# Two-layer post-norm transformer: routed experts as 23 blocks of scattered rows in place of all experts for all tokens

## What is computed

```python
x = _layernorm(x + retention(x))                       # 8 heads, decay mask, group norm, gate
x = _layernorm(x + sigmoid(x@Q(w1).T) * (x@Q(w2).T) @ Q(w3).T)   # ternary weights, 704 hidden
x = _layernorm(x + causal_softmax_attention(x))        # 16 heads of 16
# the last one, where the change is:
probs = softmax(x @ W_router.T)                        # 8 experts
rw, sel = top_k(probs, 2)
combine = zeros((T, E)).at[arange(T)[:, None], sel].add(rw)
shared_out = (silu_and_mul(x @ Ws_gate_up, 704) @ Ws_down) * sigmoid(x @ W_sgate.T)
h = silu_and_mul(einsum('th,ehi->eti', x, We_gate_up), 176)
eo = einsum('eti,eih->eth', h, We_down)
sparse_out = einsum('eth,te->th', eo, combine)         # six of eight coefficients are zero
x = _layernorm(x + shared_out + sparse_out)
```

## Time and profile before

| | us |
|---|---|
| median of 3 runs (464.0 to 464.99) | 464.88 |
| the profiled execution | 466.61 |
| its span, first to last instruction | 464.9 |
| TensorE matmuls busy | 394.7 (85%) |
| VectorE busy | 295.4 (64%) |
| ScalarE busy | 204.4 (44%) |
| GpSimd busy | 110.2 (24%) |
| mean granted TensorE clock | 0.911 |

### The profile page before, as it was taken

The page is one execution under the profiler, slowest core; times in us unless marked ns, Lnnn a source line. Parts: engine busy times, 40 slices in busy tenths (PEclk is TensorE's granted clock), DMA queues, the critical chain, the costliest instruction groups (busy, mean ns, idle before and its releaser), DMA issues.

```text
span 464.9 us, 7904 instructions
## 1 busy us (share of the span) xinstructions
PE 394.7 (85%) x3034; PEld 243.1 (52%) x3034; DVE 295.4 (64%) x656; ACT 204.4 (44%) x386; POOL 110.2 (24%) x150
## 2 busy tenths in 40 slices
PE   0958987777789877887997869999899999999996
PEld 0435656534546422233474335656446777777675
DVE  4483357976774993356469975734557968656754
ACT  4576446556126404696762044335563323222421
POOL 2345455445331001565200011012220000000000
PEclk9977889889959865899998579999999999999999
DMA  7940000133000000122000000000000000000001
GB/s 227 368 146 1 1 1 2 45 92 89 3 1 2 0 1 0 57 88 62 1 1 0 1 1 1 2 0 1 1 2 0 1 13 2 11 24 2 1 13 34
DMA packets 6856, 15.14 MB, mean 33 GB/s; under 512 B 738, under 2 KB 4130, under 8 KB 6818
## 3 DMA queue, kind: packets, MB, share of 16 engines
q1 hardware_dynamic: 6820, 14.65, 9.8%
HBM read 13.60 MB, written 1.05 MB: 32 GB/s over the span
## 4 chain that ended last, share of the span: by engine, by line
PE 58%; DVE 22%; ACT 9%; issue 6%; POOL 4%; DMA 1%; POOLq 0%; DVEq 0%
PE psum_a L640 24%; PE psum_b L640 10%; DVE arena_mixers L1290 8%; PE psum_a L776 5%; PE psum_b L848 3%; ACT arena_mixers L1050 2%; PE psum_a L838 2%; PE psum_a L880 1%; DVE arena_ffn L1332 1%; PE psum_b L830 1%; PE psum_a L875 1%; PE psum_a L647 1%; PE psum_b L788 1%; PE psum_b L760 1%; DVE arena_ffn L1329 1%
## 5 line engine op out<-in xcount | busy, mean ns | idle before, releaser
L640 PE MATMUL psum_a<-cut_weights,x_transposed 128*128 128x352 f16 (+3 forms) x774 | 134.9, 327 | 13.3 <-DVE cut_weights L1115 11.9
L640 PEld LDWEIGHTS psum_a<-cut_weights,x_transposed 128*128 128x128 f16 x774 | 75.1, 101 | 62.6 <-DVE cut_weights L1115 12.5
L1406 POOL TENSOR_TENSOR ln_rstd<-ln_var_eps,minus_half 128x1 f32<-128x1 f32 x32 | 19.7, 615 | 196.6 <-DVE ln_var_eps L1106 196.6
L1065 ACT ACTIVATE arena_ffn<-psum_a 128x352 f32<-128x352 f32 x48 | 22.3, 465 | 86.8 <-PE psum_a L640 86.8
L1423 POOL TENSOR_SCALAR_AFFINE_SELECT arena_mixers<-arena_mixers 128x256 f32<-128x256 f32 (+1 forms) x48 | 25.2, 529 | 98.0 <-ACT arena_mixers L1050 97.9
L1290 DVE TENSOR_REDUCE arena_mixers<-psum_a 128x2 f16<-128x768 f32 (+3 forms) x44 | 47.0, 1127 | 2.1 <-PE psum_a L822 2.1
L640 PE MATMUL psum_b<-cut_weights,arena_ffn 128*128 128x256 f16 (+1 forms) x408 | 46.7, 273 | 0.0
L1050 ACT ACTIVATE arena_mixers<-psum_a 128x1024 f32<-128x1024 f32 (+2 forms) x48 | 41.7, 880 | 8.0 <-PE psum_b L640 4.1
L640 PEld LDWEIGHTS psum_b<-cut_weights,arena_ffn 128*128 128x128 f16 (+1 forms) x408 | 39.1, 98 | 6.8 <-issue 1.7
L1329 DVE SCALAR_TENSOR_TENSOR arena_ffn<-arena_ffn,psum_a 128x352 f32<-128x352 f32 x48 | 24.9, 519 | 25.7 <-ACT arena_ffn L1065 14.4
L1332 DVE SCALAR_TENSOR_TENSOR arena_ffn<-arena_ffn,router,psum_a 128x176 f32<-128x176 f32 (+1 forms) x80 | 31.9, 433 | 1.7
(11 more groups left out here) (171 smaller groups left out, 640.4 us busy)
## 6 DMA issues: line engine op xcount, KB each, us to landing
stage<-in_wup SPq DMA_DIRECT2D x8, 512.0 KB, 3.6
stage<-in_wdown SPq DMA_DIRECT2D x4, 512.0 KB, 4.1
arena_ffn<-in_w SPq DMA_DIRECT2D x1, 1408.0 KB, 7.2
stage<-in_xT SPq DMA_DIRECT2D x2, 512.0 KB, 4.2
stage<-in_wqkvg SPq DMA_DIRECT2D x2, 512.0 KB, 5.2
residual<-in_x SPq DMA_DIRECT2D x2, 512.0 KB, 7.4
out<-residual SPq DMA_DIRECT2D x8, 128.0 KB, 1.7
stage<-in_wqkv SPq DMA_DIRECT2D x2, 384.0 KB, 9.0
```

The lines of the kernel that those rows point to most:

```text
L640: ins = mm(dst, lhs[k][a], rhs(k, b, col), start=(k == 0 and a == 0 and b == 0), stop=(bias_at is None and k == n - 1 and a == 1))
L1065: nc.scalar.activation(TG[:, n % 2, :], ps[:, 0, 0:MCW], ACT.Tanh, scale=0.5 * UN).then_inc(mu_tanh, 1)
L1406: g_.tensor_tensor(rstd[:, r:r + 1], veps[:, r:r + 1], half[:, 0:1], ALU.pow).then_inc(ln_rstd[layer], 1)
```

## The change

The routed experts are computed only for the rows that chose them. Shared and routed experts are separated.

- Routing: `rt` and `rc` also write into each row of `X` (now 260 wide) its token number, second choice and two weights. `rk` counts, by a matmul with a triangular matrix and one with ones, how many earlier tokens chose each expert, and makes the two places of each row. `sx` on GpSimd scatters the tile's 128 rows of 1040 bytes to DRAM twice (`expert_in`, a region of 1024 rows for each expert), by an indirect DMA. The buffer is cleared earlier by one DMA of SyncE's queue.
- `rb`, after the last tile: how many blocks of 128 rows each expert has, and for each of 23 blocks its row in DRAM (`blk_r`) and the offset of its expert's weights (`blk_u`). 23 is the largest number that can occur, and all 23 are always computed; a block beyond the last writes into a dump area.
- Blocks: SyncE waits for all scatters, loads a register per block and issues its load (`XB`), in groups of 2, 5, 8 and 8. `bx` transposes and cuts the rows, `bu` does gate and up (6 matmuls of 352 columns), `bt` transposes the hidden values, `bd` goes down (6 matmuls of 256 columns), ScalarE scales by the row's weight, and GpSimd scatters the result to `expert_out` by an indirect DMA. Four buffers each.
- Shared expert: `su` (gate and up in transposed form, 512 tokens at a time), `sh` (the cut, on ScalarE and GpSimd), `sd` (down, times the gate, added to `X`).
- End: when all scatters of the results have landed, SyncE loads both results of each token (`OL`), `os` on GpSimd adds them, `fin` adds `X` and starts the norm.
- The weights are laid out by expert (`wexp`, 1216 columns each) in 23 pieces; the last four overwrite the first layers' weights, after the last `qk`. `COST`, `LAG`, `SLACK`, `NUDGE` and `URGE` are new, so the order of all steps is.

```diff
+NBLK = NT * 2 + NE - 1
+ROW = D + 4
+SLOTS = NE * NT + NE - 1
+DEEP = 4
+GROUPS = ((0, 2), (2, 7), (7, 15), (15, NBLK))
+REC = KD * 2 * FE + 2 * D
...
     for t in range(NT):
-        add(("rt", t), ("tx", 2, t), ("split", len(PIECES) - 1), at(t > 1, ("mu", t - 2, MC - 1)))
+        add(("rt", t), ("tx", 2, t), ("split", LAST_OF["wsh"]), at(t > 1, ("rc", t - 2)))
         add(("rc", t), ("rt", t))
...
+        add(("rk", t), ("rc", t))
+        add(("sx", t), ("rk", t))
+        add(("sd", t), ("sh", t // TB, FM - 1), ("sx", t), ("split", LAST_OF["wsh"]))
+        add(("os", t), ("bd", NBLK - 1))
+        add(("fin", t), ("os", t), ("sd", t), at(t > 1, ("ln", 3, t - 2)))
...
+    for j in range(NBLK):
+        add(("bx", j), ("sx", NT - 1), ("rb",), at(j >= DEEP, ("bu", j - DEEP)))
+        add(("bu", j), ("bx", j), ("split", len(PIECES) - 1), at(j >= DEEP, ("bt", j - DEEP)),
+            at(j < NBLK - 1, ("bx", j + 1)))
+        add(("bt", j), ("bu", j), at(j >= DEEP, ("bd", j - DEEP)), at(j < NBLK - 1, ("bu", j + 1)))
+        add(("bd", j), ("bt", j), at(j < NBLK - 1, ("bt", j + 1)), ("bi", max(a for a, e in GROUPS if a <= j)))
...
+            load(7)
+            sp.dma_start(expert_in.rearrange("(j p) d -> p j d", p=P), row_init.unsqueeze(1).to_broadcast([P, SLOTS, ROW])).then_inc(rows_clear, 16)
+            for i in range(8, len(PIECES)):
                 load(i)
             for t in range(NT):
+                sp.wait_ge(sent[t], 32)
+            sp.wait_ge(tabled, 1)
+            for (a, e), here in zip(GROUPS, blocks_in):
+                for j in range(a, e):
+                    row = sp.value_load(blk_r[0:1, j:j + 1], min_val=0, max_val=(SLOTS - 1) * P)
+                    sp.dma_start(XB[:, j, :], expert_in[bass.ds(row, P), :]).then_inc(here, 16)
+            for i in range(4):
+                sp.wait_ge(returned[i], 16 * len(range(i, NBLK, 4)))
+            for t in range(NT):
+                for k in range(2):
+                    first = (k * NT + t) * P
+                    sp.dma_start(OL[:, t, k, :], expert_out[first:first + P, :]).then_inc(outs_in[t], 16)
...
+                elif kind == "bu":
+                    j = step[1]
...
+                    offset[j] = pe.value_load(blk_u[0:1, j:j + 1], min_val=0, max_val=(NE - 1) * REC)
+                    pe.wait_ge(xb_rest, j + 1)
+                    claim(step)
+                    for k in range(KD):
+                        for a, c in ((0, 0), (0, 1), (1, 0)):
+                            ins = mm(ps[:, 0:2 * FE], XBT[:, j % DEEP, a, k, :], ws[:, c, bass.ds(offset[j] + k * 2 * FE, 2 * FE)],
+                                     start=(k == 0 and a == 0 and c == 0), stop=(k == KD - 1 and a == 1))
...
+                elif kind == "bd":
+                    j = step[1]
+                    pe.wait_ge(hb_rest, j + 1)
+                    claim(step)
+                    for k, rows in ((0, P), (1, FE - P)):
+                        for a, c in ((0, 0), (0, 1), (1, 0)):
+                            ins = mm(ps[:, 0:D], HBT[0:rows, j % DEEP, a, k, :],
+                                     ws[0:rows, c, bass.ds(offset[j] + KD * 2 * FE + k * D, D)],
+                                     start=(k == 0 and a == 0 and c == 0), stop=(k == 1 and a == 1))
...
+                elif kind == "sx":
+                    t = step[1]
+                    pool.wait_ge(placed, t + 1)
+                    if t == 0:
+                        pool.wait_ge(rows_clear, 16)
+                    for k in range(2):
+                        g_.indirect_dma_start(expert_in[:, :], bass.IndirectOffsetOnAxis(ap=place_u[:, 2 * t + k:2 * t + k + 1], axis=0),
+                                              X[:, t, :], None).then_inc(sent[t], 16)
...
+                elif kind == "bd":
+                    j = step[1]
+                    pool.wait_ge(blk_out, j + 1)
+                    g_.indirect_dma_start(expert_out[:, :], bass.IndirectOffsetOnAxis(ap=blk_to[:, j:j + 1], axis=0),
+                                          OB[:, j % 4, :], None).then_inc(returned[j % 4], 16)
+                elif kind == "os":
+                    t = step[1]
+                    pool.wait_ge(outs_in[t], 32)
+                    g_.tensor_tensor(OL[:, t, 0, :], OL[:, t, 0, :], OL[:, t, 1, :], ALU.add).then_inc(summed, 1)
```

More of the change, by code:

```diff
@@ L304, in schedule @@
             times = engine_times(step)
-            start = max([end[x] - (2.0 if step[0] == "md" and x[0] == "mt" else 0.0) for x in need[step]]
+            start = max([end[x] + LAG.get((x[0], step[0]), 0.0) for x in need[step]]
                         + [free[times[0][0]]])
@@ L366 @@
 NTH = occurrences()
[L367 removed]
+LAYER = {"dn": 1, "fin": 3}
 def psum_places():
```

493 lines of the change are left out of this document (340 added, 153 removed), and 98 rows, old and new, of tables (COST, NUDGE).

## The result

The changed kernel takes **481.28 us** (median of 4 runs, 481.03 to 482.08) against 464.94 for the kernel before in the same comparison: a ratio of 1.0346, 95% interval 1.032 to 1.0373. It is slower by 3.5%. The forecast was 455. The time lies inside the range of 434 to 484, but on the other side of the kernel before. The profiled execution took 481.53 us, its span is 479.8.

The account below looks back on a forecast made before the run. PE work was taken to bound the kernel from 272 us on, dependency chains before. 272 + 82.3 other PE work + 12 idle + 46.2 blocks + 18.4 register loads + 3 clock + 21.3 tail gave 455 us, range 434 to 484.

Parts of the forecast that it names:

- The start at 272: End of the row maxima of layer-1 attention's second half; reordered schedule of the first 240 us taken as unchanged, ±3 us.
- after 272, where DVE is half idle: Four late weight cuts, 1.38 us each on DVE, mostly after 272, costed at nothing; +5.5 if inside 252 to 272.
- PE work besides the blocks, 82.3: From 272 on: 33.7 us remaining old work, 31.1 `su`, 16.0 `sd`, 1.5 counting matmuls.
- the block stage will have gaps: Reason for adding 3 us (0 to 12) for a lower granted clock while the expert blocks run.
- The last `pv` at 317: Attention half b=1 ends 45 us after 272; its 24 exponentials on ScalarE, 21 us, are the lower bound.
- Routing of four tiles, 41 us: From last `pv` at 317 to first block at about 358: 7.5 us per tile on DVE, plus scatters, landings, register loads.
- Register loads, 18.4: On PE's queue ahead of each block: load and address arithmetic at 0.8 us for 23 blocks, range 0 to 39 us.
- Rival (a): Everything overlaps: register loads hide (14 us less), idle 6 us less; 435, up to 448 us; chance 0.23 for 432 to 448.
- The blocks, 46.2 + 18.4 + 3 = 67.6: Block stage: 23 blocks of 2.0 us on PE, plus register loads and 3 us for the clock.
- The tail, 21.3: After the last block matmul: POOL is the bound at 1.4 us a tile, 11.2 for eight; 16.6 us more than before.
- rival (c): POOL bounds the block stage if a scatter takes over 2.8 us; 482 us at 4 us each; chance 0.11 with beyond.
- Rival (b), 481: Register loads cost PE 1.7 us a block (39 us), clock +5; 481 us; chance 0.28 for 464 to 485, milder forms included.

Follow-up runs that it names:

- e2: The changed kernel with all steps up to the last qk of attention half b=1 in the order of the kernel before; 470.42 us, ratio 1.0117 to the kernel before.
- e10b: e5 plus shared-expert gate-and-up fill steps and the last norm's scaling on ScalarE, with four late weight cuts moved between pv steps; 473.28 us, ratio 1.0194.
- e3: Like e2, but the old order is held up to the last row maximum, so the four late weight cuts stand behind it; 476.88 us, ratio 1.0238.
- e6: e2 with scatters of tiles 0 to 3 behind the last pv and the shared expert's first-half cut on VectorE instead of GpSimd; 473.43 us, ratio 1.0169.
- e5: e2 with the last tile's routing, counting, block table and scatter moved ahead of the shared expert's second-half gate-and-up steps; 466.18 us, ratio 0.9999.
- e4: The changed kernel without register loads on PE, block j using weights of expert j mod 8 at fixed addresses; 479.92 us, ratio 1.0329.
- e8: The changed kernel with 19 blocks instead of 23, leaving out four that write only into the dump area; 471.51 us, ratio 1.0137.
- e7: The changes of e5 and e6 together, plus every second addition of the tail moved from GpSimd to VectorE; 471.23 us, ratio 1.01.
- e1: The kernel before with only the 9.4 MB clearing DMA added behind load 7 on SyncE's queue; 465.21 us, ratio 1.001.
- e11: e5 with the shared expert's down product of tile 3 moved behind the last tile's coefficients, where PE waited; 463.74 us, ratio 0.9971.

## Why the forecast was wrong, point by point

**The start at 272, "unchanged plus or minus 3": wrong, +13.2.** This is the step that turned the sign. The change moved every tuned offset of the planner, and I took the new order of 240 us of untouched work as neutral without following it. The order could be read from the code: the plan is worked out when the kernel is built, and it puts the first FFN step at place 120 instead of 101. e2 restores before's order and gets back 10.7 us. In e2 3.2 us of the 13.2 stay, 0.5 to 3.2 in the six runs with this order. The late cuts stand inside the row maxima there; I had bounded that at +5.5 and then set it to zero, and e10b measures it at 4.9 us of that stage. What I gave as the place where they cost nothing, "after 272, where DVE is half idle", left out ScalarE: there they cost 0.8 us each (e10b), or 1.5 when they stand together (e3: 6 us).

**PE work besides the blocks, 82.3: the count was right, the price was not (+11.0).** I priced every matmul at full clock and put 3 us for the clock on the block stage, where it was 0.98. It fell in the stages before, where the waits are: 0.83 between last `pv` and first block. The largest single item is `su`: the 144 matmuls of L974 are busy 36.7 us, 31.1 forecast. The row that shows why is the 24 matmuls in 7.98 us against 5.34, 0.33 and 0.22 us each: at a granted clock of 0.50 in the first part, the lower of its two levels (1.2 GHz), and at 1.00 (2.4 GHz) later. The sentence that "the block stage will have gaps" was the wrong way round: gaps come where a chain of small operations runs, not where 23 equal steps are queued.

**The last `pv` at 317: +5.5 beyond the later start.** The stage takes 50.5 us instead of 45. I took the 21 us of exponentials as its lower bound and the other half's pace for the rest; in fact PE is busy 42.1 of 50.5 us, with the shared expert's steps between scores and `pv`, and L974, the `su` matmuls, is the largest item of the chain between 286 and 335 us, with 22.0%. e6 rules out GpSimd's queue. Whether fewer `su` steps there would shorten the stage by their length was not tried.

**Routing of four tiles, 41 us: measured 49.2.** The mechanism was right, VectorE's chain: it is busy 34.9 of these 49.2 us. What was missing is what shares the queues with it. I had asked of the register load what stands behind it, and had not asked that of the shared expert, which I treated as filler that costs nothing. One `su` stood in front of the last tile's coefficients on ScalarE and VectorE, which waited for its matmuls, and these ran at half clock. With it moved, e5 brings the count 3.8 us sooner and the whole about 5 us. Of the idle, 12 forecast, 22.2 came.

**Register loads, 18.4: wrong by nearly all of it (e4: 0 to 2 us).** I took the longest "issue" stall of PE's weight loads as nearest row. Rival (a) had argued that the load hides behind matmuls already issued, and was right in this term. The Trainium skill's floor of 600 ns for such a load (DMA: Bandwidth & Descriptors, Latency and other measured facts) fits the first load on SyncE's queue, 0.46 + 0.18 us in e2; those behind it take 0.27 + 0.16. As a cost per block on PE it would have been wrong like mine: e4 shows about 0.09 (2.1 us of block stage by 23).

**The blocks, 46.2 + 18.4 + 3 = 67.6: measured 55.5.** Without the registers 49.2 were forecast. They follow each other 2.2 us apart; e8's 2.3 to 2.4 a block is the price of one. The four blocks that only fill the dump area cost 9.7 us, more than half of the 16 us by which the kernel lost.

**The tail, 21.3: 23.6, with the wrong engine.** The lengths of VectorE's five operations stood in the rows I quoted: 0.42 and 0.43, 0.41. With the aggregate of 0.19 and the epsilon of 0.07 they are 1.5 a tile, above GpSimd's 1.4. I had added up one engine only. I repeated the error in what I expected of e7, and e7 showed it.

**Clearing: right** (e1). **GpSimd's scatters, rival (c): wrong.** A scatter takes 0.96 us of GpSimd on the mean, 1.1 forecast:

```profile
L1644 POOL DMA_INDIRECT expert_out<-arena_mixers x23 | 22.2, 963 | 34.1 <-ACT arena_mixers L1219 33.3
```

The factor of five that rival (c) worked out from the Trainium skill's rule did not appear, in line with the exception that the same section makes: in the blocks VectorE reads at most one operand from SBUF. The 620 and 3100 ns that the rival quotes stand in another section of that page, on the bandwidth of SBUF.

**Rival (b), 481, hit the time and not the cause.** That is luck: it wanted 39 us on PE's register loads. What came instead was the late end of the row maxima, the clock and the queues before the blocks. Of its milder forms, "routing latency longer than I have it" did come, 49.2 us for 41. "PE busy from 272 on near 130 to 135" was the sign that I had named; it is 145.7 from 285.2 on.

## What to carry to other kernels

When a change replans an order, treat the new order as an edit of its own: compare where the untouched steps now stand before costing anything else, for here it was two thirds of the loss. Where a long chain of small steps must end before bulk work can start, put the bulk work behind the chain's steps in every queue it shares, and into the gaps only what is as short as the gap: in e11 such a step ran at the lower clock and cost nothing, since the engine would have waited anyway, but it gained nothing either: the table came no sooner, and the work behind it was the same. And add up every engine of a short tail, not the one that looks busiest.

## What was not expected of the hardware

A register load with 12 matmuls addressed by it cost about 0.09 us a block on a saturated PE (e4). In after the clearing wrote 9.45 MB in 45.9 us, 206 GB/s; the kernel before, with the same DMA beside it, did not notice (e1). Scatters of 128 rows of about 1 KB hold GpSimd 0.96 us each and follow each other 1.27 us apart (e6); their landing in after's tail took 2.42 us. A sum of two SBUF operands on VectorE took 0.88 us instead of 0.43 when GpSimd's own sum had started 0.12 us before it (e7). A mask of GpSimd took 2.12 us instead of 0.64 beside quantizations of VectorE (after, at 96.47).
